# A decoder layer on one core: a column of zeros in front of each head's keys, and packed bytes carried as 1024+b in fp16

## The reference

```
scores = jnp.einsum('bthd,bshd->bhts', q, k)
scores = scores * jnp.tril(jnp.ones((T, T)))
attn = jax.nn.softmax(scores / T ** 0.5, axis=-1)
out = jnp.einsum('bhts,bshd->bthd', attn, v)
```

## Time and profile before

| | |
|---|---|
| median of 3 runs | 1464.04 us |
| the profiled execution | 1464.93 us, span 1463.2 us |
| PE busy | 1418.3 us, 97% of the span |
| DVE busy | 992.6 us, 68% |
| ACT busy | 711.9 us, 49% |
| POOL busy | 386.7 us, 26% |
| granted TensorE clock | full, in all slices |

### The profile page before, as it was taken

How to read it: one execution, slowest core, us unless ns; L and a number is a source line. 1 busy time by engine, 2 the same in 40 slices (tenths; PEclk the granted TensorE clock), 3 DMA queues, 4 the chain that set the end, 5 groups by cost and what they waited for, 6 DMA issues and landing times.

```text
span 1463.2 us, 26832 instructions
## 1 busy us (share of the span) xinstructions
PE 1418.3 (97%) x8896; PEld 718.8 (49%) x8896; DVE 992.6 (68%) x2125; ACT 711.9 (49%) x1648; POOL 386.7 (26%) x703
## 2 busy tenths in 40 slices
PE   6999999999999999999999999999999999999999
PEld 4466457456645644344444444444444444444444
DVE  7796788679568868885675566666666665766533
ACT  5795289249527944345344353353353343443432
POOL 0054225305473545421121121211112112212100
PEclk9999999999999999999999999999999999999999
DMA  7554612452556601010100100001001001000011
GB/s 252 136 173 122 177 67 89 126 145 67 157 147 182 206 32 45 17 33 17 33 17 17 33 17 17 23 12 35 17 17 33 17 17 33 17 17 1 1 58 58
DMA packets 77310, 98.01 MB, mean 67 GB/s; under 512 B 8049, under 2 KB 60785, under 8 KB 76785
## 3 DMA queue, kind: packets, MB, share of 16 engines
q1 hardware_dynamic: 77168, 96.23, 21.5%
HBM read 68.94 MB, written 27.26 MB: 66 GB/s over the span
## 4 chain that ended last, share of the span: by engine, by line
PE 87%; DVE 5%; ACT 4%; issue 3%; DMA 0%; POOL 0%; DVEq 0%; ACTq 0%; POOLq 0%; SPq 0%
PE bank L888 25%; PE bank L890 25%; PE bank L889 25%; PE bank L952 3%; PE bank L973 2%; ACT prob L1269 2%; PE bank L941 2%; PE bank L982 1%; PE bank L901 1%; PE bank L1013 1%; PE bank L1028 1%; PE bank L1023 1%; DVE xt L1595 1%; ACT pk_t L1303 1%; DVE bank L1610 1%
## 5 line engine op out<-in xcount | busy, mean ns | idle before, releaser
L888 PE MATMUL bank<-xs,G 128*128 128x512 f16 x896 | 339.8, 379 | 2.1 <-DVE c L1741 0.9
L889 PE MATMUL bank<-xs,G 128*128 128x512 f16 x896 | 339.6, 379 | 0.0
L890 PE MATMUL bank<-xs,G 128*128 128x512 f16 x896 | 339.6, 379 | 0.0
L1741 DVE TENSOR_TENSOR c<-bank,c 128x512 f32<-128x512 f32 x128 | 88.1, 689 | 193.0 <-PE bank L890 193.0
L1355 ACT COPY c<-bank 128x512 f32<-128x512 f32 x192 | 111.4, 580 | 220.4 <-PE bank L890 215.5
L888 PE MATMUL bank<-Wd,hid 128*128 128x512 f16 x512 | 194.1, 379 | 2.8 <-DVE X L1795 2.8
L889 PE MATMUL bank<-Wd,hid 128*128 128x512 f16 x512 | 194.0, 379 | 0.0
L890 PE MATMUL bank<-Wd,hid 128*128 128x512 f16 x512 | 194.0, 379 | 0.0
L751 POOL TENSOR_TENSOR c<-c,m 128x512 f32<-128x512 f32 x64 | 82.4, 1288 | 388.5 <-ACT c L1355 388.5
L1795 DVE SCALAR_TENSOR_TENSOR X<-bank,col,X 128x512 f32<-128x512 f32 x128 | 95.3, 749 | 101.6 <-PE bank L890 101.5
L1610 DVE CUSTOM_DVE_ANT_0 bank<-bank,mask,col 128x128 f32<-128x128 f32 (+3 forms) x256 | 139.2, 548 | 21.3 <-PE bank L941 12.1
(11 more groups left out here) (196 smaller groups left out, 2397.4 us busy)
## 6 DMA issues: line engine op xcount, KB each, us to landing
stack<-qk_dram SPq DMA_DIRECT2D x128, 128.0 KB, 3.3
sc_in<-scale_t SPq DMA_DIRECT2D x30, 384.0 KB
qk_dram<-qk SPq DMA_DIRECT2D x32, 256.0 KB, 3.1
packed_t<-pk_t SPq DMA_DIRECT2D x32, 192.0 KB, 2.0
pk_in<-packed_t SPq DMA_DIRECT2D x30, 192.0 KB
X<-in_x_dram SPq DMA_DIRECT2D x4, 1024.0 KB, 6.1
pk_in<-L_ffn_gate_W_packed_dram SPq DMA_DIRECT2D x16, 256.0 KB, 2.8
pk_in<-n_L_ffn_up_W_packed_dram SPq DMA_DIRECT2D x16, 256.0 KB, 3.1
```

The costliest lines, as they stand in the source:

```text
L888: pe.matmul(o, lhs(0), rhs(0), start=first, stop=False, skip_group_check=onto)
L889: pe.matmul(o, lhs(0), rhs(1), start=False, stop=False, skip_group_check=onto)
L890: return pe.matmul(o, lhs(1), rhs(0), start=False, stop=stop, skip_group_check=onto)
L1741: nc.vector.tensor_tensor(dst[:], bank[at][:], dst[:], ALU.add).then_inc(comb, 1)
```

## The change

The column of zeros. Each head's keys get two columns in front, both zero, and a row of 514 instead of 512 columns (the second only keeps the row's length even). For units with i < 3 the scores start one column earlier, so bank column 0 holds 0, `exp` gives exp(0 - max) in column 0 of `prob`, and its accumulated sum holds one masked key already. `e_zero` and its instruction go; the denominators and the masked values read column 0 of `prob`. The transposes start at column 1. `exp` now waits, from the third unit on, for the denominators and masked values of two units before, because they read what it overwrites.

The bytes. POOL adds 1024 while converting, so that a byte b is the fp16 number 1024 + b, whose low eight bits are b. ACT copies pairs of them as 32-bit words, DVE as fp16. The bits above do not reach the masks of `unpack_part`.

```diff
-        stack = sb("stack", [P, 2, HEADS, T], F16)
+        stack = sb("stack", [P, 2 * HEADS * T + 2 * HEADS], F16)
+        queries = stack[:, 0:HEADS * T].rearrange("p (h t) -> p h t", h=HEADS)
+        keys = stack[:, HEADS * T:].rearrange("p (h t) -> p h t", h=HEADS)
...
+        beyond = [int(i < TT - 1) for i in range(TT)]
...
-                        sp.dma_start(stack[32 * part:32 * part + 32, which, 4 * c:4 * c + 4, :],
+                        sp.dma_start((queries, keys)[which][32 * part:32 * part + 32, 4 * c:4 * c + 4, 2 * which:2 * which + T],
...
+            pool.wait_ge(w_lo, W_PARTS)
+            nc.gpsimd.memset(keys[:, :, 0:2], 0.0).then_inc(zero_keys, 1)
...
-                nc.gpsimd.tensor_copy(pk_16[:, a], pk_in[:, a].bitcast(U8).rearrange("p (c four) -> p c four", four=4)[:, :, 0]).then_inc(pk_conv, 1)
+                nc.gpsimd.tensor_scalar(pk_16[:, a], pk_in[:, a].bitcast(U8).rearrange("p (c four) -> p c four", four=4)[:, :, 0],
+                                        BYTES, None, ALU.add).then_inc(pk_conv, 1)
...
             def shift(n, u, j):
                 pool.wait_ge(max_done, n * ROWS + 4 * u + j + 1)
                 if u >= 2:
                     pool.wait_ge(exp_done, n * ROWS + 4 * (u - 2) + j + 1)
-                    pool.wait_ge(e_zero_done, beyond_units(n, u - 2))
...
             def masked_values(n, u):
-                pool.wait_ge(e_zero_done, beyond_units(n, u))
+                pool.wait_ge(exp_done, n * ROWS + 4 * u + 4)
...
-                                        e_zero[:, u % 2, :].unsqueeze(2).to_broadcast([P, 4, DH]), ALU.mult).then_inc(v_zero_done, 1)
+                                        prob[:, u % 2, :, 0:1].to_broadcast([P, 4, DH]), ALU.mult).then_inc(v_zero_done, 1)
...
             def scores(n, u, j):
+                if n + u + j == 0:
+                    pe.wait_ge(zero_keys, 1)
...
-                pe.matmul(bank[j][:, 0:wide[i]], stack[:, 0, h, P * i:P * i + P], stack[:, 1, h, 0:wide[i]],
+                pe.matmul(bank[j][:, 0:wide[i] + beyond[i]], queries[:, h, P * i:P * i + P], keys[:, h, 2 - beyond[i]:2 + wide[i]],
...
-                    mm = pe.transpose(turn_bank(slot)[:, P * k:P * k + P], prob[:, u % 2, j, P * k:P * k + P], ident[:])
+                    at = P * k + beyond[i]
+                    mm = pe.transpose(turn_bank(slot)[:, P * k:P * k + P], prob[:, u % 2, j, at:at + P], ident[:])
...
-                nc.scalar.activation(prob[:, u % 2, j, 0:wide[i]], bank[j][:, 0:wide[i]], ACT.Exp,
-                                     bias=nmx[:, u % 2, j:j + 1], accum_out=den[:, u % 2, j:j + 1]).then_inc(exp_done, 1)
-
-            def exp_zero(n, u):
-
-                if u >= 2:
                     act.wait_ge(den_done, beyond_units(n, u - 2))
                     act.wait_ge(v_zero_done, beyond_units(n, u - 2))
-                act.wait_ge(shift_done, n * ROWS + 4 * u + 4)
-                nc.scalar.activation(e_zero[:, u % 2, :], nmx[:, u % 2, :], ACT.Exp).then_inc(e_zero_done, 1)
+                nc.scalar.activation(prob[:, u % 2, j, 0:wide[i] + beyond[i]], bank[j][:, 0:wide[i] + beyond[i]], ACT.Exp,
+                                     bias=nmx[:, u % 2, j:j + 1], accum_out=den[:, u % 2, j:j + 1]).then_inc(exp_done, 1)
...
-                nc.scalar.copy(pk_t[:, 0], turn_bank(pack_slot(r, 0))[:].bitcast(F16)[:, 0:HALF]).then_inc(pk_out0, 1)
+                nc.scalar.copy(pk_t[:, 0].bitcast(F32), turn_bank(pack_slot(r, 0))[:, 0:HALF // 2]).then_inc(pk_out0, 1)
...
-                nc.vector.tensor_tensor_reduce(out=bank[j][:, 0:wide[i]], in0=bank[j][:, 0:wide[i]],
+                own = slice(beyond[i], beyond[i] + wide[i])
+                nc.vector.tensor_tensor_reduce(out=bank[j][:, own], in0=bank[j][:, own],
...
-                    dve.wait_ge(e_zero_done, beyond_units(n, u))
-                    nc.vector.scalar_tensor_tensor(den_all[:, u % 2, :], e_zero[:, u % 2, :], float(T - wide[i]), den[:, u % 2, :],
+                    nc.vector.scalar_tensor_tensor(den_all[:, u % 2, :], prob[:, u % 2, :, 0], float(T - wide[i] - 1), den[:, u % 2, :],
...
-                nc.vector.tensor_copy(pk_t[:, 1], turn_bank(pack_slot(r, 1))[:].bitcast(F16)[:, 0:HALF]).then_inc(pk_out1, 1)
+                nc.vector.tensor_copy(pk_t[:, 1].bitcast(F16), turn_bank(pack_slot(r, 1))[:].bitcast(F16)[:, 0:HALF]).then_inc(pk_out1, 1)
```

More of the change, by code:

```diff
@@ L137, in decoder_layer @@
         v_beyond = sb("v_beyond", [P, TT - 1, D], F32)
-        w_raw = stack[:].rearrange("p a h t -> p (a h t)").bitcast(F32).rearrange("p (w k n) -> p w k n", w=4, k=KT)
+        w_raw = stack[:, 0:2 * HEADS * T].bitcast(F32).rearrange("p (w k n) -> p w k n", w=4, k=KT)
         xn = sb("xn", [P, TT, D], F32)
@@ L152, in decoder_layer @@
         r_den = sb("r_den", [P, 2, P], F32)
-        e_zero = sb("e_zero", [P, 2, 4], F32)
         v_zero = sb("v_zero", [P, 2, P], F32)
@@ L223, in decoder_layer @@
         c11 = [sb2(f"c11_{x}", [P, T], F32) for x in range(2)]
+        sb2("beside_zero_keys", [P, HEADS], F32)
         G[1] = sb2("G1", [P, 7, 2, 4, P], F16)
@@ L250, in decoder_layer @@
         qkv_full, qk_hi, qk_lo, v_out = (sem(n) for n in ("qkv_full", "qk_hi", "qk_lo", "v_out"))
-        vb_full, vb_out, e_zero_done, v_zero_done = (sem(n) for n in ("vb_full", "vb_out", "e_zero_done", "v_zero_done"))
+        vb_full, vb_out, zero_keys, v_zero_done = (sem(n) for n in ("vb_full", "vb_out", "zero_keys", "v_zero_done"))
         stacked = [sem(f"stacked{i}") for i in range(4)]
@@ L317, in decoder_layer @@
         AHEAD = 4
+        BYTES = 1024.0
         CONTEXT_BANK = (6, 4, 5, 7)
@@ L1499, in body @@
                             exp(n, u, j)
-                        if j == 3 and u % TT < TT - 1:
-                            exp_zero(n, u)
                         if j == 3 and u % TT < 2:
```

## The result

The changed kernel takes 1478.84 us (median of four runs, 1478.19 to 1479.34), against 1464.32 for the kernel before on the same chip: ratio 1.0096, 95% interval 1.0083 to 1.0109. It is 14.5 us slower; 3.2 us faster was forecast, and the range ended at 1466.5. The profiled execution has a span of 1476.5 us, 13.3 more than before.

A forecast was written before the change was run, and what follows sets the result against it. Each 14.27 us group was bound by TensorE for 4.5 us, then ScalarE for 9.7. Small exponentials 3.1, extra column −0.1 and passes' ends 0.2 gave 3.2 us off the 1464.04 median: 1460.8 us, range 1456.0 to 1466.5.

The forecast's parts named there:

- the one on GpSimd: GpSimd's byte conversion, 96 times: stays at 0.40 us with the addition, covered by 6.4 us free in a group.
- rival D: VectorE's repacking copy or GpSimd's conversion slower: 4.8 or 5 us lost less 3.1 gained, time 1466; chance 0.08.
- Small exponentials: ScalarE, three a group: two removed on the path save 0.19 us a group, 3.1 us over 16 groups.
- The coupling: ScalarE's shorter repacking copy: 0 by itself, but without it the 0.10 us saved at 230.55 is lost to the negation.
- ScalarE's copy at 0.48 us: ScalarE's repacking copy as 384 words: 0.48 us in place of 0.80, costed at 0 by itself.
- VectorE's unchanged: VectorE's repacking copy keeps two-byte elements and its 0.56 us; upper bound 0.40 more each, 4.8 us lost.
- Shifted operands at 0: TensorE's keys starting at an odd half-word in a group's first three units: cost 0, upper bound 1.27 us a group.
- rival C: Odd half-word starts slow TensorE's reads of keys: a group 0.5 us or so longer, 8 us, time 1472; chance 0.09.
- Waits at 0: ScalarE's exponentials, from a pass's third unit, waiting for denominators and scaled values of two units before: already met, 0.
- transfers and the filling of the columns hidden: Keys' transfers in 1028-byte rows cost 0; GpSimd's single memset of the zero columns is hidden unless over 10 us.
- Rival A: ScalarE is the bound throughout, so its full saving of 8.5 us counts: time 1455.5, groups under 13.9 us; chance 0.13.
- Rival B: No gain: TensorE's side does not move up, the saving at 230.55 is lost; 0 to 1.5 us, time 1463; chance 0.20.

The follow-up runs named there:

- addition_alone: The kernel before with GpSimd's 96 byte conversions done as an addition of 0 in place of a copy, nothing else changed: 1470.49 us, ratio 1.0037.
- copy alone: The kernel before with the byte edit made by byte copies and ScalarE's shorter repacking copies, without the column of zeros: 1464.12 us, ratio 0.9998.
- low_bytes: The changed kernel with GpSimd copying bytes into the low bytes of a tile filled once with 1024.0, in place of the addition: 1461.55 us, ratio 0.9977.

## Why the prediction was wrong

The step that failed is the one on GpSimd: "I take 0.40. The cover: GpSimd has 14.27 − 7.82 = 6.4 us free in a group." The bounds were 0.397 and 0.80. I chose the lower one by the row of the same shape, whose operation was another; the measured 848 ns lies beyond the upper one. The Trainium skill, "GPSIMD Engine Reference", section "Elementwise — side-by-side cycle accounting", was read as making the addition free. The runs say 848 against 397 ns, and 1070 with a second operation, and the measurement decides.

The size of one instruction explains 5.6 us: that is addition_alone, and it agrees with the 5 us at which rival D priced a conversion of 0.80, and with its mechanism, the late third negation of the third unit (0.49 us a group measured, 0.3 forecast). What D lacked is 10.5 more, from the 0.12 us on either side of the conversion; the shorter copies give back 2 to 3 of it, which leaves the 13.8 of the bytes alone. No term of the prediction, and no rival, had the 0.12 us. Nor did the prediction ask how long GpSimd takes from negation to negation, against the pace of the rows. The kernels that differ from before in the conversion alone, ordered by that pair:

| pair, us | kernel | time, us |
|---|---|---|
| 0.49 (232.69 to 233.18 in its trace) | before | 1464.0 to 1464.9 |
| 0.97 | addition of 0, 1 or 2, product with 1 | 1470.5 to 1471.1 |
| 1.05 | constant from a tile | 1473.5, 1474.0 |
| 1.20 | 1024 in the instruction, old copies | 1481.0, 1481.8 |
| 1.42 | 1024 and −1024 | 1494.6 |

At 0.49 us the pair is hidden. At 0.97, just above the pace of 0.92 to 0.94, a group pays once, for the negation that has the masked values in front of it as well. Beyond it a growing number of pairs pays in full: the step from 0.97 to 1.20 us cost 10.5 us, or 46 times 0.23, and the next 0.22 us cost 13, or 60 times. There are 96 conversions, so by this estimate about half of them and then more lie on the path. The 6.4 us free in a group were real, and stood for the most part in the wrong place. In before, from the third unit's first negation to the one behind the fourth unit (231.11 to 237.33), GpSimd is busy for 4.68 of 6.22 us. So 1.5 us are free where the six conversions stand, against 6 x 0.45 = 2.7 us that the addition puts there; the other 4.9 lie where no conversion is.

The other steps, one by one:

- *Small exponentials, 3.1 us; with ScalarE's copy as what lets the second unit's share through.* Right in sum, and in part by luck. Column alone 1.75 us, copy alone 0.4 (interval 1.3 either way), both together 3.4; 3.2 was forecast. By the groups the copy was under-priced: the column alone takes 0.10 us off a group, as forecast, the copy alone some 0.11 where the step had 0, and both 0.27 where it had 0.19. The exponential at 231.34 was held by the negation, so whatever moves the negation up gains there, with the small exponentials or without. The coupling is the 0.06 us by which both exceed the sum of each; most of the effect is plain addition. In low_bytes the first and the last repacking copy lie 425.0 us apart (84.8 to 509.8) in place of 428.8, so 3.8 us less, of which the opening, 0.6 longer in the profiled execution, takes some back; the openings of the other traces differ as much, so no cause is shown for it.
- *ScalarE's copy at 0.48 us:* 0.48. *VectorE's unchanged:* 555 ns.
- *Shifted operands at 0, rival C:* products of 129 columns take 229 ns, those of 128 columns 227, and those of 385 columns 334 where 384 took 331. C is refuted; its time of 1472 would have been nearer, for a reason that isn't there.
- *Waits at 0, transfers and the filling of the columns hidden:* the column alone is faster than before, so they are.
- *Rival A* (the groups of ScalarE's full saving, under 13.9): not reached in either kernel with byte copies, 13.93 to 13.96. *Rival B's* mechanism is in part what the column alone shows: without the shorter copy the saving at 230.55 is lost, and a group gains 0.10 us in place of 0.19.

What stays open: why the written 1024 costs the gaps and 2.0 doesn't; constants between the two were not tried. The tile kernels show only that the gaps go when the constant is read from memory, not what in the instruction makes them. Nor is it shown by a run that ScalarE and VectorE, rather than TensorE, set the pace of 0.94.

## What to carry to other kernels

An engine with 45% free time is no cover for an instruction that stands in front of a short one on which others wait. Count the free time only in the stretch where the instruction stands. Compare the time from one such short instruction to the next, with everything that stands between them, with the pace at which they are asked for, and price the longer instruction from the point where that time exceeds the pace. Before a copy gets arithmetic on GpSimd, see whether a copy into part of an element, over a constant written once, does the same. And when a change joins two edits, time each alone: here one of them hid a gain of the other. Where the time can't tell a small gain, the length of the groups in the trace may.

## What the hardware showed unexpectedly

- On GpSimd a conversion of 128x256 bytes to fp16 takes 397 ns as a copy and 848 as a `tensor_scalar` with one operation (additions of 0, 1 and 2, a product with 1), 1070 with two, 936 with its constant in a tile. A byte copy into every second byte takes 399.
- With the constants 0.0, 1.0 and 2.0 written in the instruction it starts 0.15 us behind the start of a negation of 0.19; with 1024.0, in a sum or in a product, it starts 0.27 behind it, and negation to negation takes 1.20 us in place of 0.97, while the duration is the same to 4 ns. Only the idle column of the group (8.1 us) and the starts in order of time show it.
- A moving operand that starts at an odd half-word cost TensorE nothing that the trace shows: 229 ns for 129 columns against 227 for 128.
